# A graph layer on TensorE: odd groups of edges summed in a second part of the array, b3 put into layer 3's bank, and a new order of the start

## The reference

```python
h = jnp.maximum(_layernorm(x, axis=-1), 0.0)
# in the layer, with x = h:
agg_edge = jax.ops.segment_sum(edge_attr, dst, num_segments=12500)   # 12500 x 48
collected = jnp.concatenate([h, agg_edge], axis=1)                   # 12500 x 176
h1 = jax.nn.silu(collected @ W1 + b1)                                # 256
h2 = jax.nn.silu(h1 @ W2 + b2)                                       # 256
return x + (h + h2 @ W3 + b3)                                        # 12500 x 128
```

## Time and profile before

| | us |
|---|---|
| median of 3 runs | 367.86 (367.75 to 369.88) |
| time of the profiled execution | 369.57 |
| its span | 367.8 |
| TensorE busy (matmul) | 347.2 |
| VectorE, ScalarE, GpSimd busy | 260.8, 203.1, 32.6 |

### The profile page before, as it was taken

The page is one execution under the profiler, slowest core; times in us unless marked ns, Lnnn a source line. Parts: engine busy times, 40 slices in busy tenths (PEclk is TensorE's granted clock), DMA queues, the critical chain, the costliest instruction groups (busy, mean ns, idle before and its releaser), DMA issues.

```text
span 367.8 us, 11752 instructions
## 1 busy us (share of the span) xinstructions
PE 347.2 (94%) x4336; PEld 327.8 (89%) x4337; DVE 260.8 (71%) x630; ACT 203.1 (55%) x377; POOL 32.6 (9%) x44
## 2 busy tenths in 40 slices
PE   1488999999999999999999999999999999999995
PEld 1387999999999999999999999999999999999994
DVE  6864866976687667866796669766876688666652
ACT  7543466555655566456645565556555654566471
POOL 4011101110111001110111011101110011101100
PEclk9996999999999999999999999999999999999999
DMA  4953756454555455455635554545554555551111
GB/s 136 295 158 83 219 152 177 131 167 134 175 134 165 127 173 168 131 138 172 182 115 152 165 174 123 169 133 175 137 163 127 172 153 149 138 170 28 27 27 47
DMA packets 78757, 52.96 MB, mean 144 GB/s; under 512 B 2482, under 2 KB 78348, under 8 KB 78738
## 3 DMA queue, kind: packets, MB, share of 16 engines
q1 hardware_dynamic: 78738, 52.70, 50.3%
HBM read 46.29 MB, written 6.40 MB: 143 GB/s over the span
## 4 chain that ended last, share of the span: by engine, by line
PE 93%; DVE 4%; issue 2%; POOL 1%; ACTq 0%; DVEq 0%; POOLq 0%; ACT 0%
PE agg_ps L836 41%; PE z L899 14%; PE z L880 7%; PE z L888 6%; PE z L882 6%; PE z L869 3%; PE z L864 3%; PE z L870 3%; PE z L865 3%; PE z L866 3%; PE tp L849 3%; DVE farthest L522 1%; PE z L774 1%; DVE window L505 0%; DVE rel_rows L518 0%
## 5 line engine op out<-in xcount | busy, mean ns | idle before, releaser
L836 PEld LDWEIGHTS agg_ps<-onehot,raw 128*48 128x48 f32 x3128 | 147.8, 128 | 7.3 <-issue 3.6
L836 PE MATMUL agg_ps<-onehot,raw 128*48 128x42 f32 x3128 | 151.1, 217 | 3.3 <-issue 3.3
L714 DVE TENSOR_TENSOR out_t<-z,resid 112x512 f32<-112x512 f32 (+1 forms) x28 | 19.4, 692 | 84.6 <-PE z L899 84.6
L558 DVE TENSOR_TENSOR onehot<-window,rel 128x1176 f32<-128x1176 f32 (+1 forms) x56 | 76.9, 1375 | 0.7
L425 ACT ACTIVATE xn<-x_t,nmr,rstd 112x128 f32<-112x128 f32 (+1 forms) x112 | 46.2, 483 | 36.6 <-DVE nmr L550 29.8
L899 PEld LDWEIGHTS z<-w,h 128*112 128x112 f32 (+1 forms) x448 | 51.7, 176 | 5.3 <-issue 4.5
L377 POOL TENSOR_TENSOR rstd<-vareps,minus_half 112x4 f32<-112x4 f32 (+1 forms) x28 | 28.2, 1008 | 312.0 <-DVE vareps L542 312.0
L899 PE MATMUL z<-w,h 128*112 128x128 f32 (+1 forms) x448 | 54.4, 274 | 0.9 <-ACT h L446 0.9
L446 ACT ACTIVATE h<-z,b2c 128x448 f32<-128x448 f32 (+1 forms) x56 | 32.4, 631 | 26.5 <-PE z L888 26.5
L880 PE MATMUL z<-h_hi,w_hi 128*128 128x448 f32 (+1 forms) x112 | 43.5, 389 | 0.0
L385 ACT ACTIVATE agg_ps<-zeros 48x512 f32<-48x512 f32 x28 | 16.5, 592 | 45.4 <-DVE agg_carry L668 45.4
(11 more groups left out here) (89 smaller groups left out, 341.4 us busy)
## 6 DMA issues: line engine op xcount, KB each, us to landing
raw<-in_edge_attr_dram SPq DMA_DIRECT2D x55, 672.0 KB, 4.6
x_t<-in_x_dram SPq DMA_DIRECT2D x27, 224.0 KB, 2.9
out_dram<-out_t SPq DMA_DIRECT2D x27, 224.0 KB, 2.5
dst_rows<-in_dst_dram SPq DMA_DIRECT2D x1, 768.0 KB
raw<-in_edge_attr_dram SPq DMA_DIRECT2D x1, 480.0 KB, 4.0
out_t<-in_L_gnn_W_dram SPq DMA_DIRECT2D x1, 256.0 KB, 7.0
x_t<-in_x_dram SPq DMA_DIRECT2D x1, 192.0 KB
out_dram<-out_t SPq DMA_DIRECT2D x1, 192.0 KB
```

Source lines behind the costliest of these rows:

```text
L558: return dve.tensor_tensor(onehot[:, slot, 0:n * PER, :], window[:, :].unsqueeze(1).broadcast_to([P, n * PER, WINDOW]), cols.unsqueeze(2). ...
L836: mm = pe.matmul(banks[0:ED, bass.ds(offsets[k], WINDOW)], raw[0:rows, slot, k, j, :], onehot[0:rows, slot, k * PER + j, :], start=False, ...
```

## The change

It has several parts, made together.

- **Sums.** The groups are dealt into 29 batches of 14 that begin four groups before their tile (`SHIFT`), so that a batch ends where its tile's last groups would have been closed. Within a batch, groups alternate: the even ones are summed as before at tile position (0, 0), the odd ones at tile position (0, 64), into partitions 64 to 111 of another bank (`stage`), each pair of groups with fixed columns there. The four matmuls of an even group and of the odd group after it alternate. ScalarE copies the staging bank to SBUF after each batch (`stage_sums`), and GpSimd adds each odd group's 48 x 42 sums to `agg_carry` at a column read from a register (`add_odd`), three groups early, four later. `carry_over` waits for the early ones.
- **b3.** ScalarE writes b3 into layer 3's bank before the layer's matmuls, which then add to it; VectorE's addition of b3 goes.
- **x** has 4 buffers in place of 2, and loads are issued earlier; the loop is unrolled 4 times.
- **Banks and order.** Layers 1 and 2 share their two banks (`z`). TensorE's step i is now layer 2 of tile i-2, layer 1 of tile i-1, sums of batch i+1, layer 3 of tile i-2, transposes of tile i. The orders of VectorE, ScalarE and SyncE follow it, and the output of tile i-3 is finished in step i.
- **Start.** The first 128 groups' `dst` are loaded and placed first, and their offsets are ready before the rest; the first batch is summed before the other rows are transposed. Sixteen matmuls on the identity stand in the start. The flag for `general_path` is read after the second batch.

```diff
+    SLOT = 8
+    PAIRS = GPT // 2
+    STAGED = PAIRS * WINDOW
+    SHIFT = EARLY + 1
+    NB = NT + 1
...
+        def odds_of(b):
+            if not isinstance(b, int):
+                return range(1, GPT, 2)
+            return range(SHIFT + 1 if b == 0 else 1, min(GPT, NG + SHIFT - b * GPT), 2)
+        def odds_added(b, n):
+            return n if isinstance(b, int) and b == 0 else b * HALF - SHIFT // 2 + n
...
-            sp.wait_ge(s_dst, 64)
-            for half in range(2):
-                load_edges(0, 0, half)
+            sp.dma_start(first_i[:, 0:FULL_ROWS], rows[:, :, 0], allow_slow_non_contiguous=True).then_inc(s_first, 16)
+            sp.dma_start(dst_rows[:, 0, :], rows[:, 0, :]).then_inc(s_dst0, 16)
...
+            load_edges(0, 0, 0)
+            sp.dma_start(dst_rows[:, 1:FULL_ROWS, :], rows[:, 1:FULL_ROWS, :]).then_inc(s_dst, 16)
...
+            def nodes_of(b):
+                odd = odds_of(b)
+                _, nodes = nc.values_load_multi_w_load_instructions(
+                    odd_row[0:1, bass.ds(b * SLOT, len(odd))], engines=[mybir.EngineType.Pool],
+                    min_val=0, max_val=NT * TILE + OVER - WINDOW,
+                    skip_runtime_bounds_check_because="a valid group's first node is a node, else it is the centre")
+                return nodes
+            def add_odd(b, parity, nodes, early):
+                odd = odds_of(b)
+                for n, k in enumerate(odd):
+                    if (k < 2 * EARLY) != early:
+                        continue
...
+                    wait(pool, s_odd, odds_added(b, n))
+                    into = agg_carry[:, bass.ds(nodes[n], WINDOW)]
+                    pool.tensor_tensor(into, staged[:, parity, k // 2, :], into, ALU.add).then_inc(s_odd, 1)
+            def step(i, turn):
+                parity = turn % 2
+                if has(i, -1, NB):
+                    nodes = nodes_of(i + 1)
+                if has(i, -1, NT):
+                    rstd_of(i + 1, 1 - parity)
+                if has(i, -1, NB):
+                    add_odd(i + 1, 1 - parity, nodes, True)
+                    add_odd(i + 1, 1 - parity, nodes, False)
...
+            def stage_sums(t, parity):
+                act.wait_ge(s_summed, 2 * t + 2)
+                if not isinstance(t, int) or t > 1:
+                    act.wait_ge(s_odd, odds_added(t - 1, 0))
+                act.activation(staged[:, parity].rearrange("d k w -> d (k w)"),
+                               stage[ROW2:ROW2 + ED, 0:STAGED],
+                               ACT.Copy).then_inc(s_staged, 1)
+            def seed_b3(t):
+                np_ = nodes_p(t)
+                act.wait_ge(s_begun, 1)
+                wait(act, s_out, t)
+                act.activation(z3[0:np_, :, :], b3r[0:np_, :].unsqueeze(1).broadcast_to([np_, PER, D]),
+                               ACT.Copy).then_inc(s_seeded, 1)
-            def step(i, parity):
+            def step(i, turn):
+                parity = turn % 2
                 if has(i, 1, NT):
                     relu(i - 1)
+                    split_agg(i - 1)
+                if has(i, 2, NT):
+                    activate2(i - 2)
                 if has(i, 1, NT - 2):
                     act.wait_ge(s_carried, i)
                     clear_bank(1 - parity)
                 if has(i, 1, NT):
-                    split_agg(i - 1)
-                if has(i, 0, NT):
-                    normalize(i, parity)
-                if has(i, 2, NT):
-                    activate2(i - 2)
-                if has(i, 1, NT):
                     activate1(i - 1)
+                if has(i, 0, NT) and not (isinstance(i, int) and i == NT - 1):
+                    normalize(i, turn)
+                if has(i, -1, NB):
+                    stage_sums(i + 1, 1 - parity)
...
-            dve.wait_ge(s_pool_const, 11)
+            dve.wait_ge(s_pool_const, 2)
             link(dve.tensor_scalar(window[:, :], window_i[:, :], -REACH, None, ALU.add),
                  dve.tensor_copy(g["centre"][:, :], centre_i[:, :]))
...
-            def add_b3(t, parity):
...
             def step(i, turn):
+                if has(i, -2, NB) and not first:
+                    make_onehot(i + 2, parity, 0)
                 if has(i, 1, NT):
                     carry_over(i - 1, 1 - parity)
+                if has(i, 3, NT):
+                    finish(i - 3, 1 - parity)
                 if has(i, 1, NT):
                     relu_lo(i - 1)
                     agg_lo(i - 1)
...
+            for _ in range(WARM0):
+                pe.matmul(tp[:, 0:P], ident[:, :], ident[:, :], start=True, stop=True)
...
+            def batch_of(b):
+                if not isinstance(b, int):
+                    return 0, GPT
+                return (SHIFT if b == 0 else 0), min(GPT, NG + SHIFT - b * GPT)
...
+            def sum_tile(b, parity, offsets):
+                first, last = batch_of(b)
+                wait(pe, s_staged, b)
+                wait(pe, s_clear, min(b + 1, NT) if isinstance(b, int) else b + 1)
+                for k in range(first, last, 2):
...
                     for j in range(PER):
+                        for side in range(min(2, last - k)):
...
+                            if side == 0:
+                                mm = pe.matmul(banks[0:ED, bass.ds(offsets[(k - first) // 2], WINDOW)], edges, into,
+                                               start=False, stop=True, skip_group_check=True, tile_position=(0, 0))
+                            else:
+                                pair = k // 2
+                                mm = pe.matmul(stage[ROW2:ROW2 + ED, pair * WINDOW:(pair + 1) * WINDOW], edges, into,
+                                               start=(k == first and j == 0), stop=True, skip_group_check=True,
+                                               tile_position=(0, ROW2))
...
+            def step(i, turn):
+                if has(i, 2, NT):
+                    offsets = layer2(i - 2, i + 1 if has(i, -1, NB) else None)
+                elif has(i, -1, NB):
+                    offsets = offsets_of(i + 1)
                 if has(i, 1, NT):
                     layer1(i - 1)
+                if has(i, -1, NB):
+                    sum_tile(i + 1, 1 - parity, offsets)
                 if has(i, 2, NT):
                     layer3(i - 2)
                 if has(i, 0, NT):
                     transposes(i, parity)
-                if has(i, -1, NT):
-                    sum_tile(i + 1, 1 - parity, offsets)
-                if has(i, 1, NT):
-                    layer2(i - 1)
```

More of the change, by code:

```diff
@@ L113, in gnn_kernel @@
         centre_i = sb("centre_i", [P, ROWS], I32)
+        first_i = sb("first_i", [P, ROWS], I32)
         g = {n: sb("g_" + n, [P, ROWS]) for n in (
-            "base", "middle", "centre", "drift", "ok1", "ok2", "ok3", "valid", "invalid",
-            "tile", "tilet", "tile_half", "pair", "parity", "offset", "offset2", "offset3",
-            "at_centre", "instead", "placed", "shift")}
+            "base", "middle", "minus_middle", "centre", "tilet", "tile", "tile_half", "pair", "parity",
+            "begin", "in_tile", "at_centre", "other", "if_before", "if_behind", "from_centre",
+            "drift", "place", "before", "behind", "moved1", "moved2", "moved3", "ok1", "ok2", "ok3",
+            "valid", "invalid", "far", "chosen", "placed", "shift", "kept", "node")}
         rel = sb("rel", [P, NG, PER])
-        offset_row = sb("offset_row", [1, ROWS * P], I32)
+        even_row = sb("even_row", [1, NB * SLOT], I32)
+        odd_row = sb("odd_row", [1, NB * SLOT], I32)
         any_invalid = sb("any_invalid", [1, 1], I32)
@@ new lines, in _ @@
+            link(dve.tensor_scalar(g["tile"][:, :], g["tilet"][:, :], MAGIC, -MAGIC, ALU.add, ALU.add))
+            link(dve.tensor_scalar(g["tile_half"][:, :], g["tile"][:, :], 0.5, -0.25, ALU.mult, ALU.add),
+                 dve.tensor_scalar(g["begin"][:, :], g["tile"][:, :], float(TILE), None, ALU.mult))
+            link(dve.tensor_scalar(g["pair"][:, :], g["tile_half"][:, :], MAGIC, -MAGIC, ALU.add, ALU.add),
+                 dve.tensor_tensor(g["in_tile"][:, :], g["centre"][:, :], g["begin"][:, :], ALU.subtract))
@@ new lines, in _ @@
+            row_sets = ((P, slice(0, FULL_ROWS)), (LAST_G, slice(FULL_ROWS, ROWS)))
+            dve.wait_ge(s_first, 48)
+            link(*[dve.tensor_copy(g["base"][0:r, c], first_i[0:r, c]) for r, c in row_sets])
+            link(dve.tensor_scalar(g["middle"][:, :], g["base"][:, :], REACH, None, ALU.add),
+                 dve.tensor_tensor(g["drift"][:, :], g["base"][:, :], g["centre"][:, :], ALU.subtract),
+                 dve.tensor_tensor(g["place"][:, :], g["base"][:, :], g["begin"][:, :], ALU.subtract))
@@ new lines, in _, with offsets_into @@
+            dve.wait_ge(s_small0T, 1)
+            def offsets_into(b, first, last, many=1):
+                g0 = b * GPT - SHIFT + first
+                at, to = first // 2, -(-last // 2)
```

(14 more changed lines are left out.)

576 lines of the change are left out of this document (334 added, 242 removed).

## The result

Four runs of the changed kernel gave a median of 308.41 us (307.8 to 309.4), four of the kernel before beside them 367.81: a ratio of 0.838, with a 95% interval of 0.834 to 0.842. The prediction was 313 us, with a range of 298 to 352. The profiled execution took 308.38 us with a span of 306.5, against the span of 367.8 before.

The account below looks back on a forecast made before the run. TensorE, busy for 94% of the span and carrying 93% of the chain, was taken as the bound. Start 31, 25 periods of 10.15 and end 28.2 summed to 313 us against a span of 367.8; range 298 to 352.

Parts of the forecast that it names:

- S: TensorE's sums stage of one period, 112 pairs of weight load and matmul: 3.0 us in place of 5.16.
- both tiles independent: Lower bound for a pair of weight load and matmul in the sums: 23 ns, half of 46.
- The dispatch bound of 34 ns: Upper bound on TensorE's time per pair in the sums from dispatch, measured with a slow engine: 34 ns or less.
- The period above TensorE's own: Steady period: ScalarE's list, 8.0 us plus 1.7 idle and small waits, makes about 10.1 against TensorE's 9.9.
- GpSimd's adds: Chain from sums to layer 1's fourth matmul: adds 0.25 us each, 4.0 in all, hidden with 1.3 to spare.
- VectorE "in no chain": VectorE's work per tile falls from 9.3 to 8.6 us, in no chain, with 1.5 us of slack at 10.1.
- Register reads "nothing, as long as the queue holds": Reads of 7 offsets amid layer 2, behind queued matmuls, cost nothing; else 2.47 us of "issue" bounds them.
- The start: Before the steady periods: first sums at 11 us, batch 2's sums at 31 in place of 40.37, ends 28 and 36.
- the prediction's other sign of being wrong: The forecast is wrong if TensorE falls to its half clock in the steady part.
- No overlap: In the sums, loads stay in line and tile position only names columns: 351 to 361 us, chance 0.13.
- A chain takes over: Staging copy, adds or ScalarE's list hold TensorE each period: period 11 to 11.5, 334 to 347 us, chance 0.16.
- GpSimd shutting VectorE out: Each of seven adds stops VectorE for its length: slower, 457 us at 1.01 us an add, chance 0.05.

Follow-up runs that it names:

- experiment 1: The changed kernel with the odd groups' sums also at tile position (0, 0), so without the second column tile: 365.74 us.
- experiment 5: The changed kernel with GpSimd's adds one column wide in place of 42, same count, waits and signals: 305.58 us, ratio 0.831 to the kernel before.
- experiment 7: The changed kernel with VectorE computing the low part of the transposed tile before it finishes tile i-3: 310.11 us, ratio 0.844 to the kernel before.
- experiment 4: The changed kernel with b3 added by VectorE again and not written into layer 3's bank by ScalarE: 324.6 us, ratio 0.884 to the kernel before.
- experiment 3: The kernel before, in its own order, with six of every fourteen groups summed in the second column tile and their sums left unused: 334.95 us.
- experiment 10: The changed kernel with GpSimd's early adds ahead of its power and VectorE's first one-hot half behind the carry, finish and low parts: 308.51 us.
- experiment 12: The changed kernel as it is, timed and traced again: 308.76 us, ratio 0.840 to the kernel before.
- 6 to 10: Five variants of the changed kernel with GpSimd's, VectorE's or ScalarE's work reordered: 310.78, 310.11, 313.85, 311.04 and 308.51 us.

## Why the prediction was right, point by point

The forecast was 313 us and the measured time 308.41, and its main mechanism is shown by experiment 1. That the total came so near is in part luck: TensorE's own period was 9.47 us in place of 9.9, which alone makes 25 periods 10.8 us shorter, and a slow first period, in no term, took 2.7 of that back. By its terms: start 31, measured 32.9 (+1.9); 25 periods of 10.15, measured 9.85 (-7.6); end 28.2, measured 27.4 (-0.8). The span comes to 306.5 in place of 313, and the profiled execution lies 1.9 us above its span.

**The sums.** S was taken as 3.0 us, 27 ns a pair, and is 2.51, 22.6 ns: the lower bound of "both tiles independent", to the nanosecond. The reason for staying above it, that the two passes of a matmul go to the same tile in order, was mistaken: each tile keeps its own 45 ns while the other works in turns with it. The dispatch bound of 34 ns was loose too. The mechanism held; this term was mis-sized by 0.5 us a period. Of the rule that loads overlap matmuls only in other rows, set against the rows in the prediction (the Trainium skill, "TensorE: Matmul & The Clock Gate", Part 3), nothing is seen here: both tiles use the same 128 rows, and experiment 1 shows the overlap go when the two share their columns. The factor of 2.0 is also above the 1.6 that the prediction estimated from the three tiles in the same part of the Trainium skill.

**What isn't sums.** 6.86 us were carried over; it is 6.96 (9.47 - 2.51), and 6.97 in experiment 1 (11.99 - 5.02).

**The period above TensorE's own.** The prediction added 0.3 us for ScalarE, 9.9 to 10.15. The addition was right in size, 0.28, and wrong in cause, so its size was luck. It is mostly the chain through the adds to VectorE's low part (experiment 5), with ScalarE's shared banks right behind it (experiment 7). ScalarE's list was well read: the staging copy 0.41 us (0.45 taken), b3 0.58 (0.6), idle before the relu 1.71 (1.7).

**GpSimd's adds.** 0.25 us each with the semaphore was taken; one is 0.25 to 0.27 and another 0.17 to 0.26 passes before the next, and 75 of 195 are held by VectorE. And the power stands ahead of the early adds, not behind, as the prediction put it. So the chain to the sum of tile and carry, which was to start 2.0 us or so behind the sums, starts 2.9 behind the end of the stage at 185.0. The cushion of 1.3 us covered most of that. Both errors were of the same sign, and with adds at the upper bound, 1.01 us, the cushion would have been gone.

**VectorE "in no chain".** This step failed. With 1.5 us of slack on its list it is still in the chain, as its work lies between two engines' waits: giving it back 0.69 us costs as much a period (experiment 4). Slack summed over a period says nothing of one stretch in it.

**Register reads "nothing, as long as the queue holds".** It holds in the changed kernel; with 14 offsets it holds in experiment 3 as well as in the kernel before. In experiment 10 it seems not to in eight of 23 periods, for up to 0.4 us each.

**The start.** First sums at 11.90 (11 said), batch 2 at 32.93 (31). Most of the difference is TensorE's clock, whose price stood only in the term's upper end of 36. After a wait of 4.36 us for `hT_lo`, layer 1 of tile 0 began at 28.30 and took 3.7 us, where a steady one takes 2.3 (189.82 to 192.10). Then the first period, 12.14, held two things that were in no term: a wait of 2.75 us before layer 1 of tile 1, and the half clock again after it.

```profile
41.46 0.44 PE L1053 MATMUL z<-hT_hi,w1x_hi 128*128 128x448 f32 x1 [2.75 <-ACT h L563]
...
42.33 0.58 PE L1058 MATMUL z<-agg_hilo,w1e_hi 112*128 112x448 f32 x1
42.70 0.58 PE L1059 MATMUL z<-agg_hilo,w1e_lo 112*128 112x448 f32 x1
```

The windows (columns as in the earlier trace rows) give the granted clock, the value before the last two:

```profile
27.00:30.50 3.50, 2.20 (x6) 1.99 (x7) 3.44 (x7) 1.06 (x2) 2.29 (x4) 0.50 0.54 148
41.95:45.07 3.12, 3.12 (x9) 2.34 (x7) 2.99 (x7) 2.11 (x4) 0.73 (x2) 0.50 0.02 5
```

This layer 1 took 3.6 us in place of 2.3. The wait came through the three adds of batch 2, which stood behind a power of 2.61 us in the row at 35.65. In experiment 12 the same kernel had the same power and a shorter wait, kept its clock at 1.00, and its first period took 9.74:

```profile
40.35 0.44 PE L1053 MATMUL z<-hT_hi,w1x_hi 128*128 128x448 f32 x1 [1.81 <-ACT h L563]
```

Its next period, with a gap of 1.2 us within the sums, took 10.84, so by batch 4 only 1.2 us were left of the difference. In the steady part, from 45.34 us on, the clock stayed at 1.00, so the prediction's other sign of being wrong didn't come.

**The rivals.** No overlap (351 to 361) is what experiment 1 makes of the kernel, 365.7, so its price was some 5 us low. A chain takes over: it did, at 9.75 in place of 11. GpSimd shutting VectorE out: in the steady part it is the other way round.

## What to carry to other kernels

Small matmuls that followed each other as a serial chain of load and stream gained the full factor of two here from a second column tile; the columns were free (48 of 128 used) and something cheap added the halves. Once the long stage is short, what it hid comes due: here a bank clear (0.9 to 1.0 us a period in experiment 3) and one VectorE add (0.69 us in experiment 4), for neither of which TensorE had waited before. All the rest of the change without the tile brought 2 us and the tile alone, with its uneven deal, 33; together they brought 59. To find the next bound, shorten one suspect's work with all its signals in place, as experiment 5 does, and count the periods besides reading the total. Turning the order round, as 6 to 10 do, mostly moved a wait to the next reader of the same bank or port. And profile the same kernel twice before a gain at its start or end is put down to an edit: experiment 10's 2.6 us were mostly there without it.

## What the runs showed of the hardware

- Two column tiles on the same 128 rows ran fully side by side: 45.2 ns a pair of load and matmul in each, 22.6 together. With four matmuls of one tile and then four of the other in the program it was 27.8 ns together.
- An add on GpSimd of 48 x 42 took 0.25 to 0.27 us and one of 48 x 1 0.18. A power on 112 x 4 took 1.01 us alone and 1.41 at 184.95, where VectorE's `h_lo` (L877, until 185.49) and then its one-hot instruction ran beside it.
- 74 of 195 such adds ended 0.10 to 0.15 us behind a VectorE instruction with two operands in SBUF that had begun before them, and whose own length didn't change (L708 1.38 us). In experiment 10 an add at 134.87 was there first, and VectorE's `h_lo` from 134.93 took 0.69 us in place of 0.62.
- At the start it is the other way round: VectorE's L619 (128 x 4) took 1.93 us, from 1.63 on, while GpSimd's memsets were running (1.77 to 3.52), as L505 had before.
- The granted clock was 0.50, the 1.2 GHz level, from 27.0 to 30.5 us and from 41.95 to 45.07, in layers that followed waits of TensorE of 4.36 and 2.75 us. After a wait of 1.81 us in the same place of experiment 12 it was 1.00 (40.30 to 42.58). Matmuls of 448 columns began 0.37 us apart at 0.50 and 0.21 at 1.00.
